# A graph network of nine layers on one core: the node features loaded through ScalarE's queue, and two of their five blocks transposed ahead of the first permutation

## The reference, cut to what matters

```python
def _rgcn_conv(x, weight, root, bias, src, dst, etype):
    out = x @ root + bias
    for r in range(NUM_REL):
        sel = etype == r
        deg = jnp.zeros((n,), x.dtype).at[dst].add(sel.astype(x.dtype))
        norm = jnp.where(sel, 1.0 / jnp.maximum(deg[dst], 1.0), 0.0)
        msgs = (x @ weight[r])[src] * norm[:, None]
        out = out + jax.ops.segment_sum(msgs, dst, num_segments=n)
    return out
```

## Time and profile before

| | |
|---|---|
| median of 3 runs | 1507.03 us |
| lowest and highest | 1502.5 and 1509.78 us |
| the profiled execution's own time | 1506.79 us |
| its span, first to last instruction | 1505.1 us |
| mean granted TensorE clock | 0.962 |
| TensorE busy | 1394.8 us (93%) |
| VectorE busy | 786.9 us (52%) |
| GpSimd busy | 556.2 us (37%) |
| ScalarE busy | 428.6 us (28%) |

### The profile page before, as it was taken

One profiled execution on the slowest core, in us unless ns is written; L12 is line 12 of the kernel. 1 busy time (PEld: TensorE's weight loads), 2 busy tenths in 40 slices (PEclk: granted clock), 3 DMA queues, 4 the chain that ended last, 5 costly groups with the idle time before them and its releaser, 6 DMA issues.

```text
span 1505.1 us, 22367 instructions
## 1 busy us (share of the span) xinstructions
PE 1394.8 (93%) x7674; PEld 1295.0 (86%) x7674; DVE 786.9 (52%) x1847; ACT 428.6 (28%) x928; POOL 556.2 (37%) x625
## 2 busy tenths in 40 slices
PE   5999799999999999999999899889998999788797
PEld 3676799999999999999999898879978987677784
DVE  7867655323544346564231534646374614599744
ACT  2543522101110010110100311245574334445432
POOL 8101322424242534425424242033434454345630
PEclk9989899999999999999999999999999999967799
DMA  3110111112335223342111211122102211200001
GB/s 112 53 32 24 36 37 32 58 37 74 90 95 148 64 85 110 90 126 71 55 43 51 65 48 39 47 70 63 53 22 60 87 42 37 74 1 1 1 11 52
DMA packets 57782, 86.47 MB, mean 57 GB/s; under 512 B 6447, under 2 KB 54438, under 8 KB 57563
## 3 DMA queue, kind: packets, MB, share of 16 engines
q1 hardware_dynamic: 45184, 65.82, 14.8%
q10 hardware_dynamic: 12504, 19.36, 4.2%
HBM read 83.24 MB, written 1.92 MB: 57 GB/s over the span
## 4 chain that ended last, share of the span: by engine, by line
PE 75%; DVE 14%; ACT 4%; POOL 3%; issue 3%; DMA 2%; DVEq 0%; ACTq 0%; SPq 0%; POOLq 0%
PE psum L2399 14%; PE psum L2402 13%; PE psum L2403 13%; PE psum L2416 8%; PE psum L2419 8%; PE psum L2859 5%; DVE max_scratch L2104 2%; PE psum L2517 2%; PE psum L2464 2%; POOL w_lo L908 2%; PE psum L2909 1%; PE psum L2760 1%; PE psum L2764 1%; PE psum L2765 1%; PE psum L2388 1%
## 5 line engine op out<-in xcount | busy, mean ns | idle before, releaser
L2399 PE MATMUL psum<-w_lo,xT_hi 128*125 128x384 f32 (+5 forms) x1200 | 414.3, 345 | 7.2 <-DVE x_nat L1830 2.2
L2402 PE MATMUL psum<-w_hi,xT_lo 128*125 128x384 f32 (+5 forms) x1200 | 408.5, 340 | 0.0
L2403 PE MATMUL psum<-w_hi,xT_hi 128*125 128x384 f32 (+5 forms) x1200 | 408.2, 340 | 0.0
L895 POOL CAST w_hi<-w_raw 128x384 fp32r<-128x384 f32 x190 | 105.1, 553 | 501.5 <-PE psum L2403 495.4
L2399 PEld LDWEIGHTS psum<-w_lo,xT_hi 128*125 128x125 f32 (+1 forms) x1200 | 227.2, 189 | 11.8 <-POOL w_lo L908 3.4
L2402 PEld LDWEIGHTS psum<-w_hi,xT_lo 128*125 128x125 f32 (+1 forms) x1200 | 227.1, 189 | 0.5
L2403 PEld LDWEIGHTS psum<-w_hi,xT_hi 128*125 128x125 f32 (+1 forms) x1200 | 226.5, 189 | 0.0
L1673 DVE TENSOR_TENSOR h_lo<-psum,h_hi 125x384 fp32r<-125x384 f32 (+1 forms) x120 | 66.9, 558 | 289.2 <-ACT h_hi L1068 288.2
L1068 ACT ACTIVATE h_hi<-psum 125x384 fp32r<-125x384 f32 (+1 forms) x120 | 58.9, 491 | 536.4 <-PE psum L2403 532.0
L2416 PE MATMUL psum<-h_lo,adjacency 125*125 125x384 f32 (+3 forms) x600 | 203.6, 339 | 4.1 <-DVE h_lo L1673 2.1
L897 POOL TENSOR_TENSOR w_lo<-w_raw,w_hi 128x384 fp32r<-128x384 f32 x190 | 201.5, 1061 | 15.2
(11 more groups left out here) (335 smaller groups left out, 2123.6 us busy)
## 6 DMA issues: line engine op xcount, KB each, us to landing
w_raw<-weights_dram SPq DMA_DIRECT2D x296, 192.0 KB, 2.4
score_w_raw<-weights_dram ACTq DMA_DIRECT2D x58, 192.0 KB, 2.7
x_nat<-x_dram SPq DMA_DIRECT2D x1, 1875.0 KB
x_residual<-x_dram SPq DMA_DIRECT2D x1, 1875.0 KB
score_a_rows<-L_gnn_a_src_dram ACTq DMA_DIRECT2D x8, 192.0 KB, 3.2
score_a_rows<-L_gnn_a_dst_dram ACTq DMA_DIRECT2D x8, 192.0 KB, 4.8
out_dram<-x_residual SPq DMA_DIRECT2D x4, 375.0 KB
rgcn_bias<-rgcn_bias_dram SPq DMA_DIRECT2D x1, 1125.0 KB
```

Of the source, the lines that this page charges most:

```text
L895: nc.gpsimd.tensor_copy(mem.wh[:, slot, :], mem.raw[:, raw_slot, :]).then_inc(w_hi_ready, 1)
L2399: ins = nc.tensor.matmul(o, h, wl, start=(j == 0), stop=False, skip_group_check=True)
L2402: nc.tensor.matmul(o, l, wh, start=False, stop=False, skip_group_check=True)
L2403: ins = nc.tensor.matmul(o, h, wh, start=False, stop=stop and j == k - 1, skip_group_check=True)
```

## The change: what it does

The load of `x` moves from SP's queue to ScalarE's, where it is the first instruction of all. SP waits for its landing (`x_loaded`) before it issues the biases, and with them everything behind them on that queue, the weights among them. In the plan the turns of blocks 0 and 1 stand ahead of the first batch; blocks 2 to 4 stay behind batches 4 to 6, and all low parts stay where they were. The units now take four banks in turn, 4, 5, 6 and 7, so that both early blocks have a bank for each unit.

```diff
+        FIRST_TURNS = (4, 5, 6, 7)
...
             out, roots = [], [(f, m) for f in range(2) for m in range(NB)]
+            out += [("turn", 0), ("turn", 1)]
             for b in range(BATCHES):
                 out += [("fill", b), ("perms", b)]
-                if 0 <= b - 2 < NB:
+                if 2 <= b - 2 < NB:
                     out.append(("turn", b - 2))
                 if 0 <= b - 4 < NB:
                     out.append(("lower", b - 4))
...
             for i, v in enumerate((src, dst, etype)):
                 sp.dma_start(mem.edges_i[0:BP, i, :], v.rearrange("(p t) -> p t", t=ET)).then_inc(edges_loaded, 16)
-            sp.dma_start(mem.xn[0:BP, :, :], x.rearrange("(m p) d -> p m d", p=BP)).then_inc(x_loaded, 16)
+            sp.wait_ge(x_loaded, 16)
             sp.dma_start(mem.bias0[0:BP, :, :].rearrange("p l d -> p (l d)"),
...
+            act.dma_start(mem.xn[0:BP, :, :], x.rearrange("(m p) d -> p m d", p=BP)).then_inc(x_loaded, 16)
             act.wait_ge(consts_ready, 1)
...
-                    turn_hi(0, KC, mem.xh, ACT.Copy, step[1])
+                    turn_hi(0, KC, mem.xh, ACT.Copy, step[1], FIRST_TURNS)
...
-                    turn_lo(0, KC, mem.xh, mem.xl, False, step[1])
+                    turn_lo(0, KC, mem.xh, mem.xl, False, step[1], FIRST_TURNS)
...
-                    turn(KC, of(mem.xn), 0, step[1])
+                    turn(KC, of(mem.xn), 0, step[1], FIRST_TURNS)
```

## The result

The changed kernel is slower: 1509.47 us median of 20 runs (1505.26 to 1514.93) against 1503.05 for the kernel before (1498.7 to 1509.78), ratio 1.0038 with a 95% interval of 1.0026 to 1.005. By that ratio it is 5.7 us, 3.9 to 7.5 (the two medians are 6.4 apart). The forecast was 0.8 us less; the slower rival, at 5.5 us more, is what happened.

What follows compares the result with a forecast made beforehand. TensorE alone was taken to hold the chain of waits from 19.50 to 51.28 us. The sum was 1506.79 - 2.50 (two transpose blocks) + 1.7 (later edges) = 1506.0 us, range 1501 to 1512.5.

Steps and rivals of the forecast that it cites:

- slower rival: Edge loads take turns with feature packets from the first packet, landing 8.0 us late: +5.5, 1512.3 us; chance 0.18.
- (b): When the edges land beside the features: 1.7 us late, bounds nothing to 8.0, so VectorE is ready at 21.2.
- line of 0.5%: Total time: a measurement tells little under 0.5%, 7.5 us, from no change.
- no change: Measured total within 0.5% of the kernel before, neither faster nor slower by more; chance 0.91.
- Two blocks off the chain: TensorE's permutation: two blocks of transposes removed from between batches, 2 x 1.25 = 2.50 us saved.
- Twelve transposes in the idle stretch: TensorE ahead of the permutation: 2.50 us of added transposes cost nothing if ended before VectorE's first one-hot matrices.
- The fills keep up: VectorE's one-hot fills, 2.36 us or 3.4 with a low part, keep pace with TensorE's batches of 2.52.
- The cover of the weights: Weights held behind the features land at 31.7, ScalarE wants chunk 0 at about 35.8: 4 us of cover.
- (a): When the features land: 17.9, so TensorE starts turning at 18.3 and could permute at 20.8.
- no-gain rival: Features take as long to load as before, landing at 19.75; permutation 3.0 late: +0.5, 1507.3 us; chance 0.14.
- clock rival: Twelve transposes bring TensorE's clock up from 1.2 GHz; at most 1.3 us more gained, 1504.7; chance 0.03.
- The base: Starting time of the forecast's sum: the profiled execution's 1506.79 us, span 1505.1 and 1.7 around it.

Runs made afterwards that it cites:

- the plan alone: Changed kernel's plan and four banks, but SP loads the features behind the edges as in the kernel before, without SP's wait; ratio 1.0014 to the kernel before.
- half rows: Changed kernel with the features loaded as two DMAs of half rows (1536 bytes); ratio 1.0022 to the kernel before.
- wide load at once: Changed kernel with the features loaded as 112 and 13 partitions, two DMAs on ScalarE's queue at the start; ratio 1.0045 to the kernel before.

## Why the prediction was wrong

Its step that failed is (b): "I take 1.7: the five first packets last until the full flow begins, so there is little to take turns with before it." It read a slow start as an absence. The first feature rows each held their engine, for 0.30 us on average, and 33 edge packets passed from 2.2 to 3.0 us, where the kernel before has 244 and the sentence let them flow freely up to 2.85. After that the turns were one for one, as the row it cited had shown, but with 62 edge packets to an engine left (390 less 81, over five) and not 14. At 0.139 us a pair that is 8.6 us from 3.0 on, which gives 11.6 and, with the 0.4 to the cast, 12.0; measured 12.49. The step also took its value near the low end of a bound from 0 to 8.0: rows 4 show the slow start, but no row showed what it does to another queue. Even the high end was 1.0 short, and not for the row time, as 0.121 us is lost to each feature row: by 3.0 us the edges had 81 packets through, where the kernel before has 359, and were about 1.0 us behind (278 packets at 280 a microsecond); the 62 left to an engine then lost 7.5 more, together 8.5 of the 8.98.

The slower rival had the right mechanism, and its price of 5.5 against 5.7 measured is in part luck: it has two errors that offset each other, and the stage of the profile shows 4.83. Its delay of 8.0 was 1.0 short of 8.98. And it passed the delay on in full, where 1.71 us were swallowed: from the first cast to the end of the casts it was 1.75 us before and 0.46 after, and the instruction behind them (`high_f`) gave back the other 0.42, since GpSimd was out of the way by then. The row was there to be read the earlier trace rows: 1.52 us for casting 125x80 values. The time, 1509.47, lies inside the stated range only because the range reached up to this rival; and by the prediction's own line of 0.5% it is the "no change" that got 0.91, though 20 runs tell the sign.

The other steps held. Two blocks off the chain: 2.44 us against 2.50. Twelve transposes in the idle stretch: free (2.76 us, not 2.50). The fills keep up: five batches in 12.92 us. The cover of the weights: ScalarE's split without a wait. (a) had TensorE turn from 18.3, measured 19.37; it had charged 14 edge packets to an engine between them, not 78. The no-gain rival did not come about in the changed kernel; it came in the plan alone, where the features landed at 21.9 and 2.6 us were lost in the stage. The clock rival did not either: 40 matmuls in a row took 12.92 us, 0.32 each, as at 19.50 before. The base was 1506.79, the profiled execution; the median over 20 runs is 3.7 lower, and the forecast as a time carries that.

The Trainium skill's rule of the queues in turn, a packet at a time (DMA: Bandwidth & Descriptors, "Queues, rings and completion order") was weighed and set aside for the slow start. Applied as it stands it would have given the right sign, and the trace agrees with turns, of single rows here (five and five in 0.14 us). The kernel with the wide load at once shows that it is not the whole of it: there, by the counts and if the edges still run on five engines, they get less than every second row.

## What to carry to other kernels

A second queue was no second path here. Where a large load started beside a small one on the same five engines, it delayed the small one row by row, and the price was near the number of the small one's rows on an engine times the large one's row time: 75 x 0.121 = 9.1 us against 8.98 measured, and 75 x 0.065 = 4.9 against 5.51 with half rows. On 16 engines that price did not hold. So let the small load land first, or keep both in order on one queue, and ask for more engines by the count of partitions instead. Where a bound is wide and its low end rests on what a resource seems not to do in a stretch, take the row that shows what it did when two met.

## What the runs showed of the hardware

VectorE's cast from int32 to float32 stood still until GpSimd's iota (the wide table) of 128x1024 half-precision values had ended, wherever the cast began: starts at 3.51, 3.64, 3.78 and 4.70 us, the third cast at 4.99 each time, the iota's end at 4.91. With the iota out of the way a cast took 0.20. The Trainium skill has the rule (SBUF — State Buffer, "Who interferes with whom"): the two engines share a pair of ports, the one that starts first keeps it for its whole instruction, and the other stands still; casts can be among the instructions that want it. The trace agrees, 1.52 against 0.20 us, and putting the tables first moved the sorted edges by 1.98 us on the kernel before. It also moves GpSimd's other work: beside its memset of `init_columns`, the instruction behind the casts took 0.72 us in place of 0.20, in one of two profiles of one kernel.

Three DMAs over 125 partitions leave 15 end markers, five each, so each runs on five engines. The features, also over 125, went at 0.78 MB in 6 us; as 112 and 13 partitions the same rows went at 1.06 MB in 4 us, about twice as fast, though all 16 engines were busy.
